# Expert masks for the FFN from comparisons on VectorE with a row sent through DRAM, in place of one-hot turns on TensorE

## What is computed

```python
# attention part: x = x + heads @ wo.T + wo_b
t = layernorm(x) * rsqrt(mean(layernorm(x)**2) + 1e-6) * norm_w
probs = softmax(t @ gate_w.T)                 # 8 experts
topw, topi = top_k(probs, 2); topw /= sum(topw)
h1_e = t @ w1.T + 2 * (t @ a1_e.T) @ b1_e.T   # rank 16 for each expert e
h3_e = t @ w3.T + 2 * (t @ a3_e.T) @ b3_e.T   # 512 hidden numbers
act_e = silu(h1_e) * h3_e
out_e = act_e @ w2.T + 2 * (act_e @ a2_e.T) @ b2_e.T
x = x + sum_e weights_e * out_e               # two experts for each token
```

## Time and profile before

| | |
|---|---|
| median of 3 runs | 321.02 us (320.66 to 322.10) |
| the profiled execution | 320.82 us, span 319.0 us |
| TensorE / weight loads | 298.6 us (94%) / 243.3 us (76%) |
| VectorE / ScalarE / GpSimd | 225.7 (71%) / 198.2 (62%) / 189.8 us (59%) |
| mean granted TensorE clock | 0.979 of full speed |
| DMA | 8.95 MB, mean 28 GB/s |

### The profile page before, as it was taken

One profiled execution on the slowest core, in us unless ns is written; L12 is line 12 of the kernel. 1 busy time (PEld: TensorE's weight loads), 2 busy tenths in 40 slices (PEclk: granted clock), 3 DMA queues, 4 the chain that ended last, 5 costly groups with the idle time before them and its releaser, 6 DMA issues. The chain is left out here.

```text
span 319.0 us, 4612 instructions
## 1 busy us (share of the span) xinstructions
PE 298.6 (94%) x1537; PEld 243.3 (76%) x1537; DVE 225.7 (71%) x621; ACT 198.2 (62%) x336; POOL 189.8 (59%) x170
## 2 busy tenths in 40 slices
PE   4859699999999999999999999999999999998994
PEld 3638588777787888888787888888787878786873
DVE  3977865795669756895669756895659845963475
ACT  0754966478647767478647767487647747763531
POOL 2581559927892588717892488717871489326920
PEclk9996989999999999999999999999999999999998
DMA  6720020000200011000200020000000000000000
GB/s 186 242 67 0 3 66 2 1 0 1 91 10 2 0 66 36 0 1 2 66 33 3 0 66 35 0 0 2 1 33 3 0 0 35 1 1 2 33 0 33
DMA packets 7559, 8.95 MB, mean 28 GB/s; under 512 B 1264, under 2 KB 4336, under 8 KB 7536
## 3 DMA queue, kind: packets, MB, share of 16 engines
q1 hardware_dynamic: 5664, 7.41, 7.1%
q10 hardware_dynamic: 1872, 1.26, 1.2%
HBM read 6.56 MB, written 2.10 MB: 27 GB/s over the span
## 5 line engine op out<-in xcount | busy, mean ns | idle before, releaser
L848 ACT ACTIVATE silu<-h_ps 128x512 f32<-128x512 f32 x64 | 38.2, 597 | 34.6 <-PE h_ps L577 33.4
L1128 DVE TENSOR_TENSOR act_first<-silu,h_ps 128x512 f32<-128x512 f32 x32 | 22.0, 688 | 42.9 <-ACT silu L848 23.6
L577 PE MATMUL h_ps<-um_hi,b_hi 128*128 128x512 f32 x128 | 51.4, 401 | 0.0
L577 PE MATMUL h_ps<-um_hi,b_lo 128*128 128x512 f32 x128 | 50.7, 396 | 0.0
L577 PE MATMUL h_ps<-um_lo,b_hi 128*128 128x512 f32 x128 | 50.6, 395 | 0.0
L1374 POOL TENSOR_TENSOR scaled<-act_second,ratio 128x512 f32<-128x512 f32 x24 | 31.3, 1309 | 19.0 <-DVE act_second L1128 18.8
L1345 POOL TENSOR_TENSOR heads<-e_o,rec_o 128x512 f32<-128x512 f32 (+1 forms) x9 | 14.8, 1644 | 44.9 <-DVE rec_o L1037 44.8
L1128 DVE TENSOR_TENSOR act_second<-silu,h_ps 128x512 f32<-128x512 f32 x32 | 21.3, 684 | 11.3 <-PE h_ps L577 11.3
L577 PEld LDWEIGHTS h_ps<-um_lo,b_hi 128*128 128x128 f32 x128 | 24.0, 188 | 5.8
L577 PEld LDWEIGHTS h_ps<-um_hi,b_lo 128*128 128x128 f32 x128 | 24.3, 190 | 5.2
L577 PEld LDWEIGHTS h_ps<-um_hi,b_hi 128*128 128x128 f32 x128 | 24.2, 189 | 5.2
(11 more groups left out here) (268 smaller groups left out, 809.9 us busy)
## 6 DMA issues: line engine op xcount, KB each, us to landing
x_in<-in_x_dram SPq DMA_DIRECT2D x7, 256.0 KB, 3.0
ctx_in<-in_ctx_t_dram SPq DMA_DIRECT2D x7, 256.0 KB, 3.3
out_dram<-y SPq DMA_DIRECT2D x7, 256.0 KB, 2.1
act_second<-in_w_t_dram SPq DMA_DIRECT2D x2, 256.0 KB, 5.5
act_second<-in_b_dram ACTq DMA_DIRECT2D x2, 256.0 KB, 5.0
x_in<-in_x_dram SPq DMA_DIRECT2D x2, 128.0 KB, 3.0
ctx_in<-in_ctx_t_dram ACTq DMA_DIRECT2D x2, 128.0 KB, 3.4
v_parts<-in_w_t_dram SPq DMA_DIRECT2D x1, 256.0 KB, 4.7
```

The source lines that it names most:

```text
L577: mm = nc.tensor.matmul((h1_ps, h3_ps)[s][n % 2][:], b13[w][:, s, c * P:(c + 1) * P], um[k][m][:, s, :], start=False, stop=(i == 2), skip_ ...
L848: nc.scalar.activation(silu[:, n % SILU_RING, :], h1_ps[n % 2][:], ACT.Silu).then_inc(silu_done.sem, 1)
L1128: nc.vector.tensor_tensor((act_first, act_second)[k][:, c, :], silu[:, n % SILU_RING, :], h3_ps[n % 2][:], ALU.mult).then_inc(act_done.sem, 1)
```

## The change

The first block keeps its way of making masks and ratio; what follows is for the seven others. The indices of the two experts (as floats) and the logit gap are put into one tensor `choice`, 12 numbers a token row: 4 tiles for the first expert, 4 for the second, 4 for the gap. SyncE stores it to DRAM (128 pieces of 48 bytes) and loads the 1536 numbers back to every one of the 128 partitions (`chosen`, 6 KB each, 768 KB in all). VectorE then makes each mask in one operation, by comparing `chosen` with the number of the expert to which a partition belongs (`row_expert_sb`), and ScalarE makes the ratio as the exponential of the gap's part of `chosen`. The one-hots, their spreads, the turns on TensorE and the copies out of PSUM go. The masks are now 1 and not 2, so the factor 2 moves into the operations that use them, which become scalar_tensor_tensor.

```diff
+        def chosen_part(i):
+            return chosen[:].rearrange("q (p c) -> q c p", c=CHOICE)[:, i * TILES:(i + 1) * TILES, :]
...
+            def spread_choice(n):
+                sp.wait_ge(choice_done.sem, choice_done.of(n))
+                sp.dma_start(choice_dram[n % 2].rearrange("(p c) -> p c", c=CHOICE), choice[:])\
+                    .then_inc(choice_out.sem, 16)
+                sp.wait_ge(choice_out.sem, choice_out.of(n))
+                if n > 1:
+                    sp.wait_ge(masks_done.sem, masks_done.of(n - 1))
+                    sp.wait_ge(ratio_done.sem, ratio_done.of(n - 1))
+                sp.dma_start(chosen[:], choice_dram[n % 2].partition_broadcast(P)).then_inc(chosen_in.sem, 16)
...
                 if b > 0:
                     store(b - 1)
+                if b + 1 < BLOCKS:
+                    spread_choice(b + 1)
...
-            def spread_masks(n):
-                for k in range(TOP):
-                    pe.wait_ge(silu_done.sem, silu_done.of(n - 1, 7 + k))
-                    pe.wait_ge(spread_done.sem, spread_done.of(n, k + 1))
-                    by_tile(h1_ps[k], lambda t: spread[:, k, t].rearrange("p e r -> p (e r)"),
-                            lambda t: ident_bf[:]).then_inc(masks_mm.sem, 1)
...
-                elif n == 0:
-                    pe.wait_ge(ratio_done.sem, ratio_done.of(b))
                 else:
-                    pe.wait_ge(masks_done.sem, masks_done.of(b))
+                    pe.wait_ge(silu_done.sem, silu_done.of(b - 1, 7 + n))
...
+            def exp_ratio(n):
+                sc.wait_ge(chosen_in.sem, chosen_in.of(n))
+                sc.wait_ge(scaled_done.sem, scaled_done.of(n - 1))
+                sc.wait_ge(scaled_last.sem, scaled_last.of(n - 1))
+                nc.scalar.activation(tile4(ratio), chosen_part(TOP), ACT.Exp).then_inc(ratio_done.sem, 1)
...
-                if late:
-                    spread_onehot(b + 1, 0)
-                    spread_onehot(b + 1, 1)
                 b_high(b, 2)
                 z_high(b, 1)
                 z_high(b, 2)
                 if late:
-                    mask(b + 1, 0)
-                    mask(b + 1, 1)
                     exp_gap(b + 1)
+                    exp_ratio(b + 1)
                 if early:
                     exp_o(b + 2)
                 if late:
                     um_high(b + 1, 0)
-                    ratio_turned(b + 1)
                     um_high(b + 1, 1)
...
+            def choose(n):
                 ve.wait_ge(top_l_done.sem, top_l_done.of(n))
+                for t in range(TILES):
+                    op = nc.vector.max_index(top_i[:, t, :], top_l[:, t, :], logits[:, t, :])
...
+                nc.vector.tensor_tensor(choice[:, TOP * TILES:], top_l[:, :, 1], top_l[:, :, 0], ALU.subtract)\
+                    .then_inc(gap_done.sem, 1)
...
+                nc.vector.tensor_copy(choice[:, 0:TOP * TILES].rearrange("p (k t) -> p t k", k=TOP), top_i[:, :, 0:TOP])\
+                    .then_inc(choice_done.sem, 1)
+
+            def mask(n, k):
+                ve.wait_ge(chosen_in.sem, chosen_in.of(n))
+                dst = masks[n % 2][:, k, :].rearrange("p (t c) -> p t c", t=TILES)
+                if k == 0:
+                    ve.wait_ge(row_expert_in, 16)
+                    nc.vector.tensor_scalar(dst, chosen_part(0), row_expert_sb[:, 0:1], None, ALU.is_equal)\
+                        .then_inc(masks_done.sem, 1)
+                else:
+                    ve.wait_ge(masks_done.sem, masks_done.of(n, 1))
+                    first = masks[n % 2][:, 0, :].rearrange("p (t c) -> p t c", t=TILES)
+                    nc.vector.scalar_tensor_tensor(out=dst, in0=chosen_part(1), scalar=row_expert_sb[:, 0:1], in1=first,
+                                                   op0=ALU.is_equal, op1=ALU.subtract).then_inc(masks_done.sem, 1)
...
-                    nc.vector.tensor_tensor(umf[k][:, s, :], u_bank(n, s)[:], masks[n % 2][:, k, :], ALU.mult)\
+                    nc.vector.scalar_tensor_tensor(out=umf[k][:, s, :], in0=u_bank(n, s)[:], scalar=LORA_SCALE,
+                                                   in1=masks[n % 2][:, k, :], op0=ALU.mult, op1=ALU.mult)\
                         .then_inc(umf_done.sem, 1)
...
                 if late:
                     top_logits(b + 1)
-                    top_gap(b + 1)
+                    choose(b + 1)
                 act_step(b, 5)
                 if early:
                     top_of_o(b + 2)
                     shift_o(b + 2)
-                if late:
-                    onehots(b + 1)
                 act_step(b, 6)
...
                 z_low(b, 2)
                 if late:
+                    mask(b + 1, 0)
                     mask_u(b + 1, 0)
+                    mask(b + 1, 1)
                 if early:
                     sum_exp(b + 2)
```

More of the change, by code:

```diff
@@ L153, in build_program @@
         gap = sb("gap", [P, TILES])
+        choice = sb("choice", [P, CHOICE])
+        chosen = sb("chosen", [P, P * CHOICE])
+        row_expert_sb = sb("row_expert_sb", [P, 1])
         e_gap = sb("e_gap", [P, TILES])
```

97 lines of the change are left out of this document (51 added, 46 removed).

## The result

The changed kernel takes 325.16 us (median of 4 executions, 324.99 to 326.06) against 321.0 for the kernel before: a ratio of 1.0133 (95% interval 1.0108 to 1.0159), 4.2 us slower. The forecast was 322.9, 1.9 us slower. The mechanism holds in most steps, but its size is less than half of the measured one. The profiled execution of the changed kernel is the slowest of its four (326.06 us, span 324.3), so the two traces lie 5.2 us apart and not 4.2.

What follows compares the result with a forecast made beforehand. TensorE, 94% busy, was taken as held once per block by a chain through VectorE, um_hi, GpSimd and v_lo. Five turns +0.7, block 0 +1.25, last turn 0: +1.9 us, 322.9 in all; own range 321.5 to 324.5, overall 319.9 to 330.

Steps and rivals of the forecast that it cites:

- The chain through VectorE, GpSimd and v_lo binds, TensorE's removed work is worth nothing, ScalarE's too: Steady block: v_lo, behind VectorE's stretch, um_hi and GpSimd, releases TensorE; TensorE's removed 0.96 us per block counts for nothing.
- Its sign that TensorE's wait grows by about 1 us per block: Ahead of the product of v with b2: TensorE's idle time grows about 1 us per block over 0.8 on average.
- Step 6 comes 1.11 us earlier, the stretch behind follows: VectorE, steady block: searches moved and one-hots gone, act step 6 starts at 168.22 instead of 169.33, all behind 1.11 earlier.
- The factor in scalar_tensor_tensor costs nothing: VectorE's umf and v_parts as scalar_tensor_tensor: taken as 0, at most 0.11 us each, 0.44 for four.
- The DMA is hidden: Store and load of the choice: 6.4 us together, landing at 172.3 (170.4 to 177), 2.1 us to spare.
- Block 0 pays the masks in full, +1.25: Block 0: sums wait for GpSimd's scaled product, an earlier step 6 gains nothing, both masks are added: +1.25 us.
- The masks cost 0.58 + 0.67 = 1.25 us: VectorE: first mask 0.54 plus 0.04 until umf may start, second mask 0.67 us (ends 0.60 and 0.75).
- The comparison reads with a step: Rival, chance 0.33: masks read every twelfth number, costing 0.8 to 1.07 us more per block, 328 to 330 us.
- They fit in there, so their move costs nothing: VectorE's searches, moved ahead of act step 5 and in front of the gap, fit into idle time: 0 us.
- the last turn, which was put at 0: Last turn: second mask falls into idle time, first (0.58) stands against some 0.6 gained by step 6: together 0.
- the same sum: Whole loop: five steady turns at +0.14 us, block 0 +1.25, last turn 0, together +1.9 us.

Runs made afterwards that it cites:

- turns_back: Changed kernel with the eight mask matmuls and four turns per block put back on TensorE, on constant inputs, results unread: 325.41 us.
- no_masks: Changed kernel with both mask operations of each block cut to 8 columns: 318.2 us.
- tiles_only: Kernel before, in its own order, with the change's three new tiles allocated but unused: ratio 0.9996.
- cast_act: Changed kernel with the gap back in front of the searches and the cast of the choice moved from VectorE to ScalarE: 326.1 us.
- late_b2_cast: Changed kernel with the product of v with b2 behind the next hidden step 3, gap before the searches, choice cast on ScalarE: 320.31 us.
- late_packed_pe: late_b2_cast plus the choice turned on TensorE and stored as 12 rows of 512 bytes, so masks and ratio read adjacent numbers: 315.47 us.
- packed_store: Changed kernel with the row stored number by number in 4-byte pieces, so masks read adjacent numbers: VectorE waits 42.4 us for it in seven blocks; total not given.
- steps: Changed kernel with the first mask reading every second number, second mask and ratio every third: first mask 477 ns against 476 packed; total not given.
- both: Changed kernel with the second mask moved from VectorE to GpSimd, together with the edit of cast_act: 328.15 us.

## Why the prediction was wrong in size

- **The chain through VectorE, GpSimd and v_lo binds, TensorE's removed work is worth nothing, ScalarE's too:** right (turns_back, no_masks). Its sign that TensorE's wait grows by about 1 us per block is there as well (1.44 - 0.52 = 0.92 us), but turns_back has the same wait with the work put back, so the sign was no proof. 0.74 of the 0.96 us went ahead of hidden step 0, where TensorE waits for um_lo and umf only in the changed kernel. What grew the wait ahead of L649 is then the longer chain and the quicker matmuls: tiles_only, with these alone, has 0.79 where before has 0.52.
- **Step 6 comes 1.11 us earlier, the stretch behind follows:** right; from act step 5 to the place of the first mask it is 8.07 us and was 9.19 to the first umf. 1.29 us went in all, since what follows the first pair of umf now starts 178.55 - 177.35 = 1.20 us behind it, where sum_o started 176.84 - 175.48 = 1.36 behind it.
- **The factor in scalar_tensor_tensor costs nothing:** right, umf 683 against 678 ns.
- **The DMA is hidden:** right, landed at 173.6 (forecast 172.3; its terms, 165.8 + 6.4, give 172.2), asked for at 176.6.
- **Block 0 pays the masks in full, +1.25:** right in kind; 1.63 from the first um_lo, of the 1.80 that the masks cost.
- **The masks cost 0.58 + 0.67 = 1.25 us: the first step that failed.** They cost 1.80. Packed they cost 1.16, so the sum was near for the wrong read. Packed reads take 0.63 us on average from each of the five steady turns, 0.66 from block 0 and 0.21 from the last turn: 4.0 us of the 5.1 at the last L649, both counted from the first um_lo. It was named as a rival, "The comparison reads with a step", with 0.8 to 1.07 us and a chance of 0.33, and it was this rival that came true, at a smaller price.
- **"They fit in there, so their move costs nothing": the second that failed,** in the last turn, which was put at 0 and took 1.24 us. The searches fit where VectorE idled, but they pushed the gap from in front of GpSimd's z_lo to behind its start. I had read in the earlier trace rows that the gap can be held, and had not asked at which turns the move brings it there. With the gap back in front and the cast on ScalarE, the last turn is 31.21 us, that of before 31.19. In block 0 it is the cast that is held (2.32 us), but this costs nothing: cast_act, without it, takes 49.32 us from the first um_lo to L649's product, the changed kernel 49.30.
- With both mended the same sum is 5 x (0.14 + 0.55) + (1.25 + 0.55) + 1.24 = 6.5 us, above the measured 4.9. Per steady turn it is 0.69 against 0.44: 0.18 us more went from VectorE's stretch than forecast (0.16 of it behind the first pair of umf), and tiles_only shows 0.05 us for the place of the tiles. Block 0 took 1.45 us, not 1.80, 0.2 of that because the profiled execution came to its first um_lo earlier.
- **What stays open:** no run mends both steps in the changed kernel's own order. The traces show what each is worth inside the loop; in the medians packed reads gave back 2.1 of the 4.2 us (2.5 with the wait filled), and moving the cast gave nothing, since the start, one steady turn and the tail differ by as much.

## What to carry over

Before an operation is priced by a row of the same shape, look at the step of its read: fp32 numbers 12 bytes apart or more cost 1.2 to 1.8 times the packed price, and a transposition of the small source once is cheaper than a stepped read of the large copy (late_b2_cast 320.31 us, late_packed_pe, which adds it, 315.47). When a small VectorE operation is moved, look at every turn for what GpSimd runs at its new place. Work taken from an engine that waits is worth nothing, while an order that fills the wait with the next ready step can be worth a lot: moving one product did 5 us here, more than the change had cost, and it did so with the removed work put back too. And two versions that differ in their tiles are compared with the tiles in the same place.

## What the runs showed of the hardware

- A four-column subtraction and an eight-column cast on VectorE took 2.36 and 2.32 us beside a GpSimd tensor_tensor of 2.40 us (0.16 and 0.18 alone), and um_lo of VectorE 2.31 in place of 1.16 us beside GpSimd's subtraction; the umf beside GpSimd's comparison (one input from PSUM) kept its 0.64. The Trainium skill (SBUF — State Buffer, Who interferes with whom) calls this an exclusive lock on a port pair that both share; the rows agree.
- Three unused tiles (6.2 KB per partition) made TensorE's 512-column matmuls start 228.5 ns apart on average in place of 233.0, those too whose operands lie in front of the new tiles (t_lo with w_hi: 233.4 to 227.6). Why is open.
- In nine profiled executions TensorE waited 2.1 to 3.0 us ahead of the last product of the loop. In six the granted clock was at 1.2 GHz for 3.4 to 6.8 us from there on (packed_store is one, and there it falls in every turn); in three it stayed up (the changed kernel's 2.52, steps' 2.33 and both's 2.99). With waits of 1.5 us and less it fell in two (late_packed_pe, late_b2_cast) of eleven. The length of that one wait doesn't decide it alone.
- 6 KB scattered in 1536 pieces of 4 bytes landed in 8.5 us, in 128 pieces of 48 bytes in 1.4.
